# The start of a residual MLP with per-row experts: other warm-ups, another load order, block 0 transposed by row, and fc1's second half transposed inside chunk 0

## The reference

```
h      = gelu(x @ fc1_w.T + fc1_b)                 # 256 -> 1024
shared = h @ fc2_w.T + fc2_b                       # 1024 -> 192
expert = h @ experts_w[index[row]].T + experts_b[index[row]]   # 1024 -> 64
out    = x + concatenate([shared, expert])
```

## Time and profile before

| | |
|---|---|
| median of 3 runs | 357.58 us (357.48 to 357.83) |
| the profiled execution | 357.54 us |
| its span in the trace | 355.4 us |
| PE busy | 350.9 us, 2381 matmuls |
| DVE, ACT, POOL busy | 259.5, 246.8, 235.0 us |
| first matmul of the warm-ups | 1.53 us |
| first matmul of chunk 0 | 7.19 us |
| first matmul of chunk 1 | 9.87 us |

### The profile page before, as it was taken

The page is one execution under the profiler, slowest core; times in us unless marked ns, Lnnn a source line. Parts: engine busy times, 40 slices in busy tenths (PEclk is TensorE's granted clock), DMA queues, the critical chain, the costliest instruction groups (busy, mean ns, idle before and its releaser), DMA issues.

```text
span 355.4 us, 7075 instructions
## 1 busy us (share of the span) xinstructions
PE 350.9 (99%) x2381; PEld 323.7 (91%) x2381; DVE 259.5 (73%) x498; ACT 246.8 (69%) x410; POOL 235.0 (66%) x150
## 2 busy tenths in 40 slices
PE   8999999999999999999999999999999999999996
PEld 5899899999999999999999999999999999999996
DVE  2797976968859697786968869697786968844642
ACT  4885957777678577767777678577777777666560
POOL 0179887658866586865758866576865758855471
PEclk9999999999999999999999999999999999999999
DMA  8779663533333334341533324353332230312001
GB/s 239 172 162 191 140 181 85 148 99 89 112 87 117 89 90 141 94 110 59 149 98 89 114 79 122 90 137 101 84 107 64 90 99 30 120 38 89 31 30 61
DMA packets 69981, 37.53 MB, mean 106 GB/s; under 512 B 43450, under 2 KB 69946, under 8 KB 69946
## 3 DMA queue, kind: packets, MB, share of 16 engines
q1 hardware_dynamic: 69376, 36.55, 38.1%
q10 hardware_dynamic: 570, 0.53, 0.4%
HBM read 28.68 MB, written 8.39 MB: 104 GB/s over the span
## 4 chain that ended last, share of the span: by engine, by line
PE 98%; ACT 0%; issue 0%; POOL 0%; DVE 0%; POOLq 0%; ACTq 0%
PE fc_ps L1110 40%; PE acc_ps L1166 29%; PE acc_ps L1169 15%; PE fc_ps L1086 6%; PE acc_ps L1136 3%; PE acc_ps L1189 2%; PE fc_ps L1166 1%; PE fc_ps L1052 1%; PE fc_ps L1093 1%; PE fc_ps L1169 1%; PE tr_ps L1046 0%; ACT xt L461 0%; PE tr_ps L1068 0%; ACT w1t L474 0%; DVE resid L906 0%
## 5 line engine op out<-in xcount | busy, mean ns | idle before, releaser
L395 POOL TENSOR_TENSOR ht<-gelu,ht 128x1024 fp32r<-128x1024 f32 x62 | 149.5, 2411 | 97.4 <-ACT ht L565 97.4
L1166 PE MATMUL acc_ps<-w2t,ht 128*128 128x512 f32 x448 | 162.4, 397 | 0.0
L1110 PE MATMUL fc_ps<-xt,w1t 128*128 128x256 f32 x1176 | 159.9, 284 | 0.0
L1110 PEld LDWEIGHTS fc_ps<-xt,w1t 128*128 128x128 f32 x1176 | 148.7, 189 | 5.5
L1169 PE MATMUL acc_ps<-w2t,ht 128*128 128x256 f32 x448 | 125.9, 281 | 0.0
L1166 PEld LDWEIGHTS acc_ps<-w2t,ht 128*128 128x128 f32 x448 | 84.4, 188 | 14.9
L1169 PEld LDWEIGHTS acc_ps<-w2t,ht 128*128 128x128 f32 x448 | 85.0, 190 | 0.0
L565 ACT ACTIVATE ht<-gelu 128x1024 fp32r<-128x1024 f32 x64 | 68.0, 1063 | 3.6 <-issue 0.4
L591 ACT ACTIVATE gelu<-work,b 128x512 f32<-128x512 f32 x56 | 37.3, 715 | 26.2 <-DVE work L870 26.1
L403 POOL TENSOR_TENSOR xt<-work,xt 128x1024 fp32r<-128x1024 f32 x14 | 33.8, 2417 | 14.8 <-ACT xt L554 14.8
L870 DVE TENSOR_TENSOR work<-fc_ps,work 128x512 f32<-128x512 f32 x28 | 19.4, 692 | 22.6 <-PE fc_ps L1110 21.3
(11 more groups left out here) (73 smaller groups left out, 335.6 us busy)
## 6 DMA issues: line engine op xcount, KB each, us to landing
pieces<-in_L_cond_experts_w SPq DMA_DIRECT2D x128, 64.0 KB, 2.0
out<-resid SPq DMA_DIRECT2D x31, 256.0 KB, 3.1
pieces<-in_x SPq DMA_DIRECT2D x60, 128.0 KB, 2.9
resid<-in_x SPq DMA_DIRECT2D x15, 512.0 KB, 3.5
e_bias<-in_L_cond_experts_b SPq DMA_DIRECT2D x32, 32.0 KB, 2.8
work<-in_L_cond_fc_w SPq DMA_DIRECT2D x4, 256.0 KB, 4.7
w_piece<-in_L_cond_fc_w SPq DMA_DIRECT2D x4, 192.0 KB, 5.0
resid<-in_x SPq DMA_DIRECT2D x2, 256.0 KB, 3.2
```

Of the source, the lines that this page charges most:

```text
L395: nc.gpsimd.tensor_tensor(ht[:, slot, LO, :, :].rearrange("p k t -> p (k t)"), gelu[:, q % GELUS, :, :].rearrange("p k t -> p (k t)"), ht[ ...
L1110: last = nc.tensor.matmul(fc1_ps[:, dst, j * SEQ:(j + 1) * SEQ], w1t[:, w, wv, ms], xt[:, n % 2, o, xv, :], start=(fresh and j == 0 and at ...
L1166: nc.tensor.matmul(acc.rearrange("p (v o) -> p v o", v=2), ht[:, q % SLOTS, HI, j, ts], w2t[:, :, k, fc2_columns(b)], start=(k == 0), stop ...
```

## The change

- **Warm-ups.** A new tile `warm_in` is cleared by DVE as its first instruction; PE waits for that (`warm_ready`) and does 13 warm-ups on it. It waits for the identity only behind them.
- **Loads.** fc1's first half is loaded as two transfers of two strips, 256 KB each: strips 0 and 1 by ACT where the whole was, strips 2 and 3 by SP right behind the two rows of x, each with its own semaphore.
- **x of block 0.** Bank b of `tr_ps` now holds row b with both feature halves (it was bank d, with both rows), so `x0_high(b)`, `x0_low(b)` work on one row.
- **PE's order.** Row 0 of x, strips 0 and 1 for both d, row 1, strips 2 and 3 for both d, b1, then chunk 0 with all 512 columns, with the four transposes of fc1's second half for d = 0 ahead of its last matmul, and those for d = 1 between chunk 0 and chunk 1.
- **Banks.** fc1's second half is transposed to banks 2 and 3 of `fc1_ps`; chunks 2 and 3, which write these, wait for `w1_lo`.
- **ACT and DVE.** ACT does `w1_high(1, 0)` and `w1_high(1, 1)` ahead of the gelu of chunk 0. DVE copies b1 ahead of `w1_low(0, 0)`.

```
-    WARM = 12
+    WARM = 13
...
-        def load_w1(queue, half):
-            queue.dma_start(w1_in[:, half * HALF:(half + 1) * HALF, :], w1_halves[half])\
-                .then_inc(w1_loaded[half], 16)
+        def load_w1(queue, half, part, strips):
+            cols = slice(half * HALF + strips.start, half * HALF + strips.stop)
+            queue.dma_start(w1_in[:, cols, :], w1_halves[half][:, strips])\
+                .then_inc(w1_loaded[part], 16)
+
+        def w1_ps(half, d):
+
+            return acc_ps[:, d, :] if half == 0 else fc1_ps[:, 2 + d, :]
+
+        def x0_row(v, b):
+            return xt0[:, :, v, b * SEQ:(b + 1) * SEQ]
+
+        def x0_bank(b):
+            return tr_ps[:, b, :].rearrange("p (d t) -> p d t", d=D)
...
                 sp.dma_start(resid[:, 0, ts, :], x_blocks[0][:, ts, :]).then_inc(x0_loaded[b], 16)
+            load_w1(sp, 0, 1, slice(Q // 2, Q))
 
             sp.wait_ge(x0_loaded[0], 16)
-            load_w1(sp, 1)
+            load_w1(sp, 1, 2, slice(0, Q))
...
-            load_w1(act, 0)
+            load_w1(act, 0, 0, slice(0, Q // 2))
...
-            for d in range(D):
-                x0_high(d)
+            for b in range(R):
+                x0_high(b)
             for d in range(D):
                 w1_high(0, d)
+            for d in range(D):
+                w1_high(1, d)
             act.wait_ge(b1_ready, 1)
             conv_chunk(0)
-            w1_high(1, 0)
-            w1_high(1, 1)
             conv_chunk(1)
...
-            for d in range(D):
-                x0_low(d)
+            nc.vector.memset(warm_in[:, :], 0.0).then_inc(warm_ready, 1)
+            for b in range(R):
+                x0_low(b)
+            dve.wait_ge(b1_tr, 1)
+            nc.vector.tensor_copy(b1[:, :], fc1_ps[:, 3, 0:K]).then_inc(b1_ready, 1)
             for d in range(D):
                 w1_low(0, d)
-            dve.wait_ge(b1_tr, 1)
-            nc.vector.tensor_copy(b1[:, :], fc1_ps[:, 3, 0:K]).then_inc(b1_ready, 1)
...
-                if c == 3:
-                    pe.wait_ge(b1_ready, 1)
+                if 2 <= c < 4:
+
+                    pe.wait_ge(w1_lo, c + 1)
...
+            pe.wait_ge(warm_ready, 1)
+            warm(WARM)
             pe.wait_ge(ident_ready, 1)
-            warm(WARM)
-            for b in range(R):
-                x0_banks(b)
+            x0_banks(0)
             pe.wait_ge(w1_loaded[0], 16)
             for d in range(D):
-                w1_bank(0, d)
+                w1_strips(0, d, range(Q // 2))
+            x0_banks(1)
+            pe.wait_ge(w1_loaded[1], 16)
+            for d in range(D):
+                w1_strips(0, d, range(Q // 2, Q)).then_inc(w1_tr, 1)
             pe.wait_ge(b1_loaded, 16)
             nc.tensor.transpose(fc1_ps[:, 3, 0:K], b1_in[:, :], ident[0:K, 0:K]).then_inc(b1_tr, 1)
-            first_chunk()
-            pe.wait_ge(w1_loaded[1], 16)
+            pe.wait_ge(x0_hi, R)
             for d in range(D):
-                pe.wait_ge(x0_lo, d + 1)
-                w1_bank(1, d)
+                pe.wait_ge(w1_hi, d + 1)
+                first(d, HI, HI)
+                pe.wait_ge(x0_lo, R)
+                first(d, HI, LO)
+            pe.wait_ge(w1_lo, 1)
+            first(0, LO, HI)
+            pe.wait_ge(w1_loaded[2], 16)
+            w1_strips(1, 0, range(Q)).then_inc(w1_tr, 1)
+            pe.wait_ge(w1_lo, 2)
+            first(1, LO, HI).then_inc(conv_filled, 1)
+
+            pe.wait_ge(b1_ready, 1)
+            w1_strips(1, 1, range(Q)).then_inc(w1_tr, 1)
             conv_chunk(1)
```

More of the change, by code:

```diff
@@ L92, in cond_mlp_residual @@
         ident = sbuf("ident", [P, P])
+        warm_in = sbuf("warm_in", [P, P])
         b1_in = sbuf("b1_in", [K, P])
@@ L124, in cond_mlp_residual @@
         stored = [sem(f"stored{n}") for n in range(2)]
-        w1_loaded = [sem(f"w1_loaded{n}") for n in range(2)]
+        w1_loaded = [sem(f"w1_loaded{n}") for n in range(3)]
         w1p_loaded = sem("w1p_loaded")
@@ L164, in cond_mlp_residual @@
         h_hi = sem("h_hi")
+        warm_ready = sem("warm_ready")
         b1_ready = sem("b1_ready")
@@ L375, in residual @@
                     pool.wait_ge(x0_loaded[b], 16)
-                    pool.wait_ge(x0_tr, D)
+                    pool.wait_ge(x0_tr, R)
                 else:
@@ L458, in _, with x0_high @@
         def _(act):
[L459 to L462, removed]
+            def x0_high(b):
+                act.wait_ge(x0_tr, b + 1)
+                nc.scalar.activation(x0_row(HI, b), x0_bank(b), ACT.Copy).then_inc(x0_hi, 1)
             def w1_slots(half, d, v):
@@ L472, in w1_high @@
                 act.wait_ge(w1_tr, D * half + d + 1)
-                src = (acc_ps, tr_ps)[half][:, d, :].rearrange("p (l c) -> p l c", l=2)
+                src = w1_ps(half, d).rearrange("p (l c) -> p l c", l=2)
                 nc.scalar.activation(w1_slots(half, d, HI), src, ACT.Copy).then_inc(w1_hi, 1)
@@ L705, in _, with x0_low @@
         def _(dve):
[L706 to L710, removed]
+            def x0_low(b):
+                dve.wait_ge(x0_hi, b + 1)
+                nc.vector.tensor_tensor(x0_row(LO, b), x0_bank(b), x0_row(HI, b).bitcast(FP32),
+                                        ALU.subtract).then_inc(x0_lo, 1)
             def w1_slots(half, d, v):
@@ L947, in _ @@
             w2_low(3)
-            dve.wait_ge(w1_lo, 2 * D)
+            dve.wait_ge(x0_lo, R)
             for half in range(2):
@@ L1049, in warm @@
             def warm(times):
-                bits = ident[:, :].bitcast(BF16)
+                bits = warm_in[:, :].bitcast(BF16)
                 for _ in range(times):
@@ L1056, in x0_banks, with w1_strips @@
                 pe.wait_ge(x0_loaded[b], 16)
[L1057 to L1067, removed]
+                transposes(tr_ps[:, b, :], [feature_chunk(resid[:, 0, b * T + t, :], d)
+                                            for d in range(D) for t in range(T)]).then_inc(x0_tr, 1)
+            def w1_strips(half, d, strips):
+                dst = w1_ps(half, d).rearrange("p (k q c) -> p q k c", q=Q, c=S)
+                for q in strips:
                     last = nc.tensor.transpose(
                         dst[:, q], feature_chunk(w1_in[:, half * HALF + q, :], d), ident[:, :])
-                last.then_inc(w1_tr, 1)
+                return last
             def conv_operand(j, d, v):
@@ L1089, in conv_chunk, with first @@
                 last.then_inc(conv_filled, 1)
[L1091 to L1097, removed]
-                    pe.wait_ge(x0_lo, d + 1)
[L1099 to L1103, removed]
+            def first(d, w, v):
+                return nc.tensor.matmul(fc1_ps[:, 0, :], conv_operand(0, d, w), xt0[:, d, v, :],
+                                        start=(d == 0 and w == v), stop=(d == D - 1 and w == LO))
             def product(n, g, dst, w, o, fresh):
```

## The result

The changed kernel takes 358.28 us (median of 17 runs, 357.66 to 359.63), the one before 357.76 in the same rounds (17 runs, 357.25 to 357.95): 0.52 us more, the ratio 1.0022 with a 95% interval of 1.0014 to 1.003. The runs also spread over 2.0 us instead of 0.7. The profiled execution took 358.28 us, with a span of 356.2.

What follows compares the result with a forecast made beforehand. PE, busy 99%, was taken as the bound, with only time ahead of chunk 1 winnable. Warm-ups 0.00, chunk 0's start +0.28 and hidden work -0.30 turned 357.54 into 357.5 us, range 356.9 to 358.1.

Steps and rivals of the forecast that it cites:

- "same": Whole kernel: time differs by no more than 0.2%, about 0.7 us, from the kernel before; chance 0.87.
- second rival: Strips 0 and 1 land late, between 5.0 and 5.75; each 0.1 delays everything 0.1, +0.7 at worst, 358.2; chance 0.13.
- The sum: Start up to chunk 1: 0.00 warm-ups, +0.28 for chunk 0's start, -0.30 hidden inside it, giving 357.5 us.
- so fc1's second half and everything queued on SP behind it stays where it is: SP's queue: the third issue, 0.4 to 0.5 us, ends before the wait ending at 3.51, so later loads don't move.
- They land at 5.0: ACT's load of fc1's strips 0 and 1 lands at 5.0 us, with bounds of 4.3 and 5.75.
- x's row is safely ahead: Loads: x's second row is ahead of SP's strips in the same queue, an argument against late strips.
- worth nothing by itself: Earlier transposes and high and low passes of x's first row, done by 6.2, gain nothing, as the next loads end what follows.
- The first (early strips): Strips 0 and 1 land by 4.75, chunk 1 starts at 9.5: -0.38, 357.2 us; chance 0.24.
- The third (the clock): PE's clock rises late, slowing transposes and chunk 0: +1.1 to about +3, 358.6 to 360.5 us; chance 0.07.
- The waits behind chunk 0 that were costed at nothing: Chunks 2 and 3 waiting for low parts, POOL near 19.3 (0.26 in hand), DVE's drain near 43: no cost.

Runs made afterwards that it cites:

- changed_5: The changed kernel unaltered, measured again in later rounds: +0.63 us over the kernel before, ratio 1.0026; its traced execution took 357.54 us.
- w2_waits: The changed kernel with SP holding fc2_w back until strips 2 and 3 are there: +0.82 us over the kernel before, ratio 1.0022.
- two unpaced kernels: SP's wait for x's first row removed from the changed kernel, and from it with x's rows ahead of the strips: +1.07 and +1.00 us over the kernel before.
- changed: The changed kernel as first measured, against the kernel before: +0.52 us, ratio 1.0022; its traced execution took 358.28 us.
- act_both: The changed kernel with strips 2 and 3 issued by ACT instead of SP: +0.50 us over the kernel before, ratio 1.002.
- filled: The changed kernel with five more warm-ups behind the transposes of x's first row: +1.06 us over the kernel before, ratio 1.0024.
- x_first_5: The changed kernel with both rows of x transposed ahead of strips 0 and 1: +0.17 us over the kernel before, ratio 1.0011.
- inner_rows: The kernel of inner_5 plus block 0's x transposed to banks by row and b1 copied earlier: +0.09 us over the kernel before, ratio 0.9993.
- inner_5: The kernel before with only fc1's second half transposed inside chunk 0 and what goes with that: -0.32 us against the kernel before, ratio 0.9993.
- split_only: The kernel before with only fc1's first half loaded in two transfers, PE's order as before: +0.19 us over the kernel before, ratio 1.0005.
- whole: The changed kernel with fc1's first half as one load by ACT and PE's old order up to b1: +0.15 us over the kernel before, ratio 0.9999.
- again: The changed kernel unaltered, for a second trace: +1.09 us over the kernel before; the traced execution took 359.44 us.
- cold_before: The kernel before with no warm-ups: +0.81 us over the kernel before.
- cold_after: The changed kernel with no warm-ups: +1.01 us over the kernel before.

## Why the prediction was wrong

The time, 358.28, lies 0.18 above the range, and "same" had 0.87 of the chance where the kernel became 0.15% to 0.3% slower, clear of no change though at the edge of the prediction's own line of 0.2%. The range ended at 358.1 where its own second rival is priced at 358.2. And the kernel before ran at 357.76 beside it, 0.18 above the 357.58 that the prediction had: so 0.52 of the 0.78 us between 357.5 and 358.28 is the change's.

**The sum was right for the execution that it described.** It took clock and landings of one trace of the kernel before. changed_5's trace has those, but for a second half that landed 1.0 later and yet in time, and term by term: warm-ups from 1.07 (1.00), the strips at 5.04 (5.0), x0_high(1) at 6.34 (6.32), chunk 0 at 7.57 (7.47), chunk 1 at 9.91 (9.86). The 0.1 missed at chunk 0 is that its first matmul came 0.14 us behind ACT's pass and not 0.05. It is 0.14 to 0.15 in all thirteen traces of kernels with two waits ahead of it, and 0.05 in five of seven with one, so the second wait is the likely reason. That the sum fits the fastest of twelve runs says that its terms were read rightly, not that it forecast the kernel: it described a rare draw as the usual one.

**The step that failed is "so fc1's second half and everything queued on SP behind it stays where it is".** It did not stay: with fc1's first half as one transfer the second landed at 7.5 to 8.8 in eight traces, mean 8.0; split, it landed at 8.2 to 10.1 in nine, mean 9.1 (w2_waits and the two unpaced kernels, which issue it or fc2_w at other times, left out). In the traces of this order where chunk 0 starts by 7.7, PE comes to it at 8.6 to 8.7. In the first trace of the changed kernel fifteen of the sixteen shares of that load had landed by 7.55, and the last came at 9.39. PE's transposes inside chunk 0 began at 9.43 there and at 8.82 in changed_5, so the late share cost 0.6 of the 0.77 us by which chunk 1 missed 9.86. The prediction's range for a transfer that is ordered as before had no term for this. Of the ten traces of split loads with SP's wait, PE waited for this load in four (changed, act_both, filled, x_first_5), its weight loads by 0.3 to 0.9 us: so it is a part of the loss and not all of it.

**The other step is the order.** "They land at 5.0" was right as a single value, and the second rival priced the rest: 0.1 us for each 0.1 later, as x's second row stands behind them. It got 0.13 of the chance, as if the strips' landing were one fixed unknown. It is a draw in every execution: of the ten traces of split loads with SP's wait, seven have it at 5.03 to 5.24 and three at 5.75 to 6.08, each time with x's second row late too, against the prediction's argument that x's row is safely ahead. The clock's rise is a draw as well, 3.8 to 9.8 us over twenty traces. The order before has some slack for both, since x's transposes run while fc1 is still loading; the new order puts all twelve transposes behind the strips. changed_5 against x_first_5 puts this at 0.46 us in the medians, though the runs of the two overlap widely and the difference isn't resolved.

**A term put at nothing.** The prediction had the earlier passes over x's first row "worth nothing by itself". inner_rows against inner_5 has x's banks by row, with b1's earlier copy, at +0.4, in the traces mostly as a later landing of fc1's first half, and why stays open.

Added up in medians: inside chunk 0 -0.3, banks by row and b1 +0.4, order about +0.5, warm-ups 0.0, split +0.2 (split_only) or 0.0 (x_first_5 against whole), together +0.6 to +0.8, against +0.52, +0.63 and +1.09 measured. That mixes chips, and of its terms only the +0.4 stands out from the runs' spread. What is shown is that split and order together are the loss (whole against again); how it divides between them is argued.

**The rivals.** The first (early strips) never showed: 5.03 was the earliest landing. The second (late strips) came in three of ten traces. The third (the clock) happened, in part, in both kernels; warm-ups half a microsecond earlier didn't help, and the cleared data didn't hurt. The Trainium skill's statement that transposes don't count as busy (TensorE: Matmul & The Clock Gate, Part 4) isn't borne out here: cold_before and cold_after, with no matmuls but transposes up to 8.05 and 8.44 us, had the clock up at 8.01 and 7.69. The waits behind chunk 0 that were costed at nothing (19.3, 43 us, chunks 2 and 3) cost nothing, as the near-constant distance from c1 to the end shows.

**What stays open.** Why a split transfer makes a later one late. One trace with fc2_w held back has it on time; that wasn't repeated. Why inner_rows is slower than inner_5. What sets the moment of the clock's rise wasn't found.

## What to carry to other kernels

Where the start of a kernel is a race of loads, one trace gives one draw of landing times and of the clock's rise: cost an order by what it does when each load comes 0.5 us late, and take the order in which work that is ready never stands behind work that may not be. Here the version to keep is the old kernel with only the transposes inside chunk 0, 357.28 and 357.58 us against 357.60 and 357.84, a likely gain. Test the parts of a change one by one: the one that looked free cost the most clearly. And a transfer whose own order is untouched can still land later when the ones ahead of it are cut in two.

## What the runs showed of the hardware

- The same load of 512 KB, issued at 3.4 to 3.7 us, landed at 7.5 to 8.8 us behind one transfer of fc1's first half (mean 8.0 of eight) and at 8.2 to 10.1 behind two (mean 9.1 of nine), with one of its sixteen shares up to 1.8 us behind the rest.
- The granted clock of TensorE went up anywhere from 3.84 to 9.84 us after the span's start, with warm-ups from 1.07 or 1.54 us (4.67 and 7.46 in the kernel before, unaltered); without warm-ups at 7.69 and 8.01.
- Taking away a wait that paced the loads, so that they were issued 1.3 us earlier, didn't bring fc1's second half in before 8.5 and won nothing: +1.07 and +1.00 us over the kernel before, with runs spread over 5.2 and 3.3 us.
